# A graph network's gathers: the clears between GpSimd's indirect transfers are taken out, and each transfer waits for a signal from the one before it

## What is computed

```python
h = relu(layernorm(x))
x = x + L0_gnn(h, edge_weight, edge_attr_3, edge_index, ...)   # sweep 0: a message of 32 per edge, from h[src],
                                                               # a small network of the weight, and the direction
h = relu(layernorm(x))
def gcn_conv(x, src, dst, norm, W, b):                         # sweeps 1, 2 and 3
    msg = (x @ W)[src] * norm[:, None]
    return segment_sum(msg, dst, n_nodes) + b
h = relu(gcn_conv(h, ..., W1, b1)); h = relu(gcn_conv(h, ..., W2, b2)); h = relu(gcn_conv(h, ..., W3, b3))
return x + h
```

## Time and profile before

| | |
|---|---|
| time, median of 3 runs | 5768.08 us (5767.51 to 5774.85) |
| the profiled execution, from its first to its last instruction | 5779.7 us; no other time of it is given |
| GpSimd busy | 4889.1 us, 85% of the span |
| TensorE busy (matmuls) | 4258.6 us, 74% |
| VectorE busy | 3608.0 us, 62% |
| ScalarE busy | 2702.7 us, 47% |
| DMA engines' mean rate | 69 GB/s |

### The profile page before, as it was taken

One profiled execution on the slowest core, in us unless ns is written; L12 is line 12 of the kernel. 1 busy time (PEld: TensorE's weight loads), 2 busy tenths in 40 slices (PEclk: granted clock), 3 DMA queues, 4 the chain that ended last, 5 costly groups with the idle time before them and its releaser, 6 DMA issues.

```text
span 5779.7 us, 179150 instructions
## 1 busy us (share of the span) xinstructions
PE 4258.6 (74%) x62463; PEld 3147.7 (54%) x62464; DVE 3608.0 (62%) x8469; ACT 2702.7 (47%) x6550; POOL 4889.1 (85%) x7276
## 2 busy tenths in 40 slices
PE   5777777777777777755555555889898889766666
PEld 3444444444444444444444444778787778554554
DVE  8777777777777777776666666333333334555555
ACT  4444444444444444466666666344444444433333
POOL 7888888888888888768888888688888889588886
PEclk9999999999999999955555555899989999767767
DMA  3111111111111111333332332332333333444444
GB/s 87 33 33 33 33 33 31 33 33 33 33 33 32 32 33 33 36 71 77 77 77 77 77 77 71 114 90 85 91 91 85 91 91 100 119 119 126 122 127 107
DMA packets 494970, 400.88 MB, mean 69 GB/s; under 512 B 269575, under 2 KB 454828, under 8 KB 493537
## 3 DMA queue, kind: packets, MB, share of 16 engines
q10 hardware_dynamic: 146996, 207.67, 10.6%
q0 software_dynamic: 115712, 109.02, 10.3%
q1 hardware_dynamic: 231536, 74.48, 5.9%
HBM read 375.52 MB, written 15.29 MB: 68 GB/s over the span
## 4 chain that ended last, share of the span: by engine, by line
POOL 50%; issue 40%; PE 5%; POOLq 2%; DVE 2%; DMA 1%; ACT 0%; DVEq 0%; SPq 0%
POOL rows L782 29%; POOL pause L762 21%; POOLq L761 2%; PE radial L2067 2%; PE psX L2082 1%; PE psT L2082 1%; PE sums L2153 1%; PE radial L2209 0%; DMA table<-arena 0%; PE radial L2222 0%; DMA rows<-table,idx 0%; DMA xn<-in_x 0%; POOLq L760 0%; PE radial L2008 0%; DVE rows L1827 0%
## 5 line engine op out<-in xcount | busy, mean ns | idle before, releaser
L782 POOL DMA_INDIRECT rows<-table,idx x3616 | 3636.6, 1006 | 803.0 <-POOL pause L762 483.7
L762 POOL MEMSET pause<- 128x256 f32 x3616 | 1234.8, 341 | 2.5
L1942 PEld LDWEIGHTS sums<-scratch,onehot 128*64 128x64 f32 x9408 | 789.7, 144 | 465.0 <-DVE scratch L1377 228.6
L2067 PE MATMUL radial<-arena,shared 128*32 128x96 bf16 (+1 forms) x31200 | 926.4, 266 | 154.2 <-DVE shared L1613 75.1
L1942 PE MATMUL sums<-scratch,onehot 128*64 128x264 f32 (+1 forms) x9408 | 984.1, 356 | 32.6 <-DVE scratch L1377 26.2
L2067 PEld LDWEIGHTS radial<-arena,shared 128*32 128x32 bf16 (+1 forms) x31200 | 664.8, 116 | 294.4 <-issue 72.0
L2153 PE MATMUL sums<-onehot,rows 128*128 128x80 f32 (+1 forms) x2844 | 371.0, 298 | 576.7 <-DMA rows<-table,idx 571.8
L1007 ACT CAST scratch<-radial 128x480 bf16<-128x480 f32 x860 | 476.9, 555 | 665.7 <-PE radial L2067 657.6
L1360 DVE TENSOR_TENSOR scratch<-radial,shared 128x768 f32<-128x768 f32 x784 | 743.4, 948 | 0.0
L1927 PE MATMUL radial<-shared 64*128 64x384 f32 x3136 | 730.5, 546 | 0.0
L880 ACT COPY shared<-rows 128x192 f32<-128x192 f32 x196 | 89.4, 456 | 1264.1 <-DMA rows<-table,idx 1262.9
(11 more groups left out here) (237 smaller groups left out, 5969.3 us busy)
## 6 DMA issues: line engine op xcount, KB each, us to landing
scratch<-places_d ACTq DMA_DIRECT2D x242, 800.0 KB
rows<-table,idx POOLq DMA_INDIRECT x3616
shared<-in_edge_weight SPq DMA_DIRECT2D x390, 128.0 KB, 2.9
idx<-in_src SPq DMA_DIRECT2D x451, 4.0 KB
table<-arena SPq DMA_DIRECT2D x24, 256.0 KB, 2.8
table<-arena SPq DMA_DIRECT2D x2, 1176.0 KB, 10.6
accT<-in_edge_attr SPq DMA_DIRECT2D x2, 1152.0 KB
table<-arena SPq DMA_DIRECT2D x24, 96.0 KB, 2.0
```

Of the source, the lines that this page charges most:

```text
L762: nc.gpsimd.memset(pause[:, :], 0.0).then_inc(made, 1)
L782: (pool.indirect_dma_start(rows_3[:, r, j, :] if n in (1, 3) else rows[:, r, j, 0:WIDTH[n]], None, tables[n], bass.IndirectOffsetOnAxis(ap ...
L1942: last = nc.tensor.matmul(there, onehot[:, u % 2, 4 * h + t, 0:SW], taken_from, start=(h + q + part == 0), stop=(h == 1 and q == 1 and par ...
L2067: last = nc.tensor.matmul(d, from_src[n][:, h, i, t, :], table_of(n, s), start=True, stop=True, tile_position=(0, 32 * i))
```

## The change

The tile `pause` and its clears are gone. The wait and the counting stay, under the name `after_previous`, but they stand ahead of the transfer instead of behind it, and the semaphore `made` is now raised by the transfer itself, by its argument `engine_sem`. The order in a loop becomes: register move, wait until transfer j-1 has raised `made` with the addition, transfer j, register move, and so on. The values that are waited for are those of before: 9 and the number of transfers before this one. In the peeled steps the wait is for a constant and is carried by the transfer itself.

```diff
-            pauses = pool.alloc_register("pauses")
-
-            def pause_between(step, n, u, j):
+            described_before = pool.alloc_register("described_before")
+
+            def after_previous(step, n, u, j):
 
                 if step.peeled:
                     before = TPG * (sum(GATHERED[:n]) + step.it * step.groups + u) + j
                     if before:
                         pool.wait_ge(made, 9 + before)
                 else:
-                    pool.wait_ge(made, pool.snap(pauses))
-                    pool.reg_add(pauses, pauses, 1)
-                nc.gpsimd.memset(pause[:, :], 0.0).then_inc(made, 1)
+                    pool.wait_ge(made, pool.snap(described_before))
+                    pool.reg_add(described_before, described_before, 1)
...
                         for j in range(TPG):
                             col = j % 2 * KS + j // 2
+                            after_previous(step, n, u, j)
                             (pool.indirect_dma_start(rows_3[:, r, j, :] if n in (1, 3) else rows[:, r, j, 0:WIDTH[n]], None, tables[n],
-                                                     bass.IndirectOffsetOnAxis(ap=idx[:, r, col:col + 1], axis=0))
+                                                     bass.IndirectOffsetOnAxis(ap=idx[:, r, col:col + 1], axis=0),
+                                                     engine_sem=made)
                                  .then_inc(gathered[r], 16))
-                            pause_between(step, n, u, j)
```

More of the change, by code:

```diff
@@ L61 @@
 PAD_REL = -1000.0
-PAUSE = 256
 assert NG % UNROLL == 0 and PTAIL * KS == ETAIL and PTAIL <= P and NG == 2 * NB
@@ L295, in gnn_kernel @@
         one = sb("one", [P, 1])
-        pause = sb("pause", [P, PAUSE])
         flag = sb("flag", [P, 1])
@@ L806, in gathers @@
                     pool.reg_mov(turn[u], 2 * (LOOP[n][0] // UNROLL - 1) if n else 0)
-                pool.reg_mov(pauses, 9 + TPG * (sum(GATHERED[:n]) + LOOP[n][0]))
+                pool.reg_mov(described_before, 9 + TPG * (sum(GATHERED[:n]) + LOOP[n][0]))
                 sweep(pool, body, n)
```

## The result

The changed kernel takes 6,436.6 us (median) against 5,767.8 us of the kernel before beside it: a ratio of 1.115, with a 95% interval of 1.114 to 1.117. It is slower by 11.5%, where 6,775 us (+17%) had been forecast. One of its four executions took 6,836 us, with a mean granted TensorE clock of 0.545 in place of 0.78, and is left out of the ratio.

What follows compares the result with a forecast made beforehand. GpSimd's round of transfers was taken as the bound. 912 - 20 for the loops and 127 - 14 for the peeled steps gave +1,005 us, so 6,775 us (+17%), range 6,250 to 7,350.

Steps and rivals of the forecast that it cites:

- The bound: Nearly everywhere, the time is the number of transfers times GpSimd's round, 3,616 rounds of 1.51 us in the mean.
- The handing on: In the loops, the sequencer's preparation of a transfer is uncovered: 0.80 us from end to start in place of 0.50.
- 912 - 20: Loops: 0.30 us lost in each of 3,040 rounds, 912 us, less 20 us given back at the ends of steps.
- The peeled steps: 576 transfers that carry the wait themselves: between a gain of 184 us and a loss of 127, less 14 in sweep 2.
- the upper end: Peeled steps: the sequencer waits before preparing, 0.72 us from end to start, a loss of 127 us.
- The first rival: Peeled steps: preparation hidden while the transfer waits, about -150 us in place of 127 - 14; 6,510 us, chance 0.12.
- the nearest row: Start of sweep 2: a transfer carrying its own wait for indices, GpSimd idle before it, took 0.70 us.
- The records: GpSimd's transfers, all sweeps: each record counted at 1.006 us in the mean, before and after the change.
- The signal: Each transfer raises its semaphore at the end of its record; at most 14 ns of its tail hide in the clear.
- The rivals of a late, an early and an exactly balanced signal: Late by 0.1 to 0.2: 7,100 to 7,400 us, chance 0.15; early: 4,910, 0.17; exactly 0.30 early: no change, 0.02.
- The clock: TensorE's granted clock may fall, sweep 0's group needing at most 16 us; counted as nothing, kept for the upper end.
- The value taken for the removal: Every round: the clear, 0.341 us, and the 0.16 idle behind it go, 0.50 us between records now.

Runs made afterwards that it cites:

- experiment 4: Changed kernel with the wait between transfers, its register and the transfers' signal taken out, leaving GpSimd's own order; 4,911 us, ratio 0.851 to the kernel before.
- experiment 2: Kernel before, clears and place of the wait unchanged, but each transfer also signals its end; 5,769 us, ratio 1.000.

## Why the prediction was right or wrong

The measured 6,437 us lies inside the stated range of 6,250 to 7,350, but below the 6,650 to 6,950 that the forecast gave itself, and 338 us under the forecast.

**The bound** was read rightly: the time follows GpSimd's round in the loops, over six rounds (1.25, 1.33, 1.44, 1.65, 1.70 and 2.04 us).

**The handing on** was the step that decided the sign, and it held. The forecast from one step's end in the earlier trace rows was 0.80 us from end to start; it was 0.76, since 0.70 and not 0.75 stand behind the addition. The loops were to cost 912 - 20 = 892 us, and cost 858. That they came so close is in part luck: the usual round brought 79 us less than the 912 (0.763 - 0.489 = 0.274 us in place of 0.30, times 3,040), and the longer idle times, of which 20 us were to be given back, added 25. Above all it is the long idle times once in 96 transfers (see experiment 4) that grew, from 46 to 73 us.

**The peeled steps** are where the prediction's mechanism failed. Its words were "I take the upper end", 0.72 us and a net loss of 113 us. They took 0.30, except for the first transfer of a group (0.77). With the 32 us that are given back before sweep 3, since TensorE stays the bound in the last 16 groups of sweep 2, the term is -54 us. (That stretch is 67 to 70 us in the kernels with peeled rounds of 1.44 us and more, and 94 to 102 in those with 1.25.) The error is one of 167 us. The first rival, from the rule of the Trainium skill (Perfetto Trace Analysis, DMA Instruction — SWDGE (GPSIMD)) by which such an instruction is decoded and queued before its semaphore is satisfied, described these steps; the traces agree with it (0.30 where the transfer carries the wait, 0.76 where another instruction does). So the sequencer doesn't keep every wait to itself, as the description of the kernel before has it: a wait on the transfer leaves its preparation covered. The rival's time of 6,510 us was 73 off, but that is luck: it gave the peeled steps about -150 us where they brought -54, and against these 96 us stand the 192 that the loops and the records took less than it had them. I had called the nearest row, but in it the indices' semaphore had risen 80 us before the transfer's turn came, so it could not tell waiting after preparing from waiting before it.

**The records** were taken as unchanged at 1,006 ns. They became 962: -158 us, the other half of the error. The lines of GpSimd's transfers in sweep 0, before, after, and with clears of 512 columns:

```profile
L782 POOL DMA_INDIRECT rows<-table,idx x1568 | 1599.3, 1020 | 304.7 <-POOL pause L762 240.0 <-issue 35.2 <-DMA idx<-in_src 29.6
```

```profile
L780 POOL DMA_INDIRECT rows<-table,idx x1568 | 1487.4, 949 | 1235.2 <-DMA rows<-table,idx 1158.1 <-issue 48.7 <-DMA idx<-in_src 28.5
```

```profile
L782 POOL DMA_INDIRECT rows<-table,idx x1568 | 1499.6, 956 | 302.7 <-POOL pause L762 240.6 <-issue 32.7 <-DMA idx<-in_src 29.4
```

Sorted by their place in the group (transfers 41 to 1,500), the mean records of sweep 0 are 972, 975, 1277, 955, 970, 1102, 954 and 953 ns before, and 939 to 941 after, but for one of 976. It is the third and the sixth that were long, each in nine groups of ten. The timeline of the kernel before at such a third transfer, and at the sixth of the same group:

```profile
1256.34 0.76 DVE L1326 TENSOR_TENSOR shared<-arena,rows 128x576 f32<-128x576 f32 x1 [4.24 <-ACT shared L887]
1256.60 1.32 POOL L782 DMA_INDIRECT rows<-table,idx  x1 [0.16 <-POOL pause L762]
...
1261.24 0.34 DVE L1338 TENSOR_TENSOR shared<-shared 128x192 f32<-128x192 f32 x1
1261.31 1.11 POOL L782 DMA_INDIRECT rows<-table,idx  x1 [0.16 <-POOL pause L762]
```

The record at 1256.60 begins while VectorE's product of line 1326 runs, the one at 1261.31 while its difference of line 1338 runs; both instructions read two operands from SBUF. Of the 429 records of sweep 0 over 1 us, 378 begin so. All 190 that begin under line 1326 are long, and each ends 0.83 us after VectorE's instruction has ended, whatever that had left between 0.20 and 0.68 us; the same holds for 188 of the 189 under line 1338. The 759 that begin under line 1360, which reads `radial` from PSUM, have the usual 953 ns. Nor is a record longer when line 1326 begins within it (in the changed kernel 167 of transfers 41 to 1,500, 940 ns in the mean). So a record that begins under one of the two waits until it is over. Line 1326 comes after the group's last arrival, so it falls at the same place of the round each time, and another round puts it elsewhere: in the changed kernel 4 records begin under it and 15 under the other. No kernel was run that moves VectorE's work alone, and what the two engines share isn't shown.

About 11 ns a record stand apart, 40 of the 158 us: the usual record is 942 to 945 ns without clears and with a clear of one column, and 949 to 953 with longer ones. The other 119 us are what the records exceed the usual length by (191 us before, 72 after).

**The signal** comes at the end of the record, as assumed: the addition starts 0.03 us behind it, and experiment 2 shows that it costs nothing. The rivals of a late, an early and an exactly balanced signal are out.

**The clock.** TensorE's mean granted clock in sweep 0 went from 0.92 to 0.87, with its busy share there down from 77% to 71%, and its busy time over the span rose from 4,259 to 4,389 us. As forecast it wasn't the bound, but for the end of sweep 2, and no time is put down to the clock.

The sum, then: 1,005 forecast; -34 for the loops, -167 for the peeled steps with their end, -158 for the records and 2 for the rest make 648, the measured 647.

**The value taken for the removal** was right only as an account. That 0.50 us stands between two records does not mean that it can be had: 0.30 of it is needed with nothing in between, and the most that the removal alone could have brought was 0.19 a round. Experiment 4, which takes out clears and waits alike, gains 861 us, 0.24 a round, because the records and the long idle times got shorter too.

## What to carry to other kernels

Ask of every wait where its instruction stands, and what the sequencer still has to do once it passes. A wait behind the expensive instruction lets the next one be prepared under cover; the same wait ahead of it, on an instruction of its own, uncovers the whole preparation, here 0.46 us in each of 3,040 rounds. If the order has to be kept, let the instruction itself carry the wait (4,949 us here in place of 6,437), or wait one further back (4,984).

Preparation that is hidden everywhere shows at the few places where the engine ran dry. One such row at a step's end gave the price in the loops to within 0.04 us a round; but a row in which the semaphore had already risen says nothing of how a wait behaves.

## What the runs showed of the hardware that I had not expected

Between two indirect transfers in a row GpSimd was idle 0.30 us, both without a wait and with one that the transfer carried or that was met a transfer earlier. A clear of one column in between is free (1.25 us a round in both), and one of 256 columns costs 0.19 us and not 0.33. A transfer that carries the wait for the previous transfer starts as early as one that doesn't wait. A transfer's record that began while VectorE worked on two operands in SBUF (lines 1326 and 1338) ended 0.83 us after that instruction, 0.07 to 0.55 us late. So taking clears of 256 columns to 512 made the 3,616 records shorter by 129 us in all, 100 of them in sweep 0, where only 19 of them began under these two lines in place of 379.
